# First stage of a fused kernel on one core: differences of the running sums move from GpSimd to ScalarE, and the mask of C B gets two buffers

## What is computed

```python
zxbcdt = x @ W_in;  z, xBC, dt = split(zxbcdt)
xBC = silu(conv4(xBC));  xh, B, C = split(xBC)         # 8 heads of 64, state 64
dt = softplus(dt + dt_bias);  dA = dt * -exp(A_log)
A_cum = cumsum(dA)                                     # per head, along the tokens
L[l, s] = exp(A_cum[l] - A_cum[s])  for l >= s, else 0
Y_diag  = sum_s (C[l] . B[s]) * L[l, s] * (x[s] dt[s])
states  = B, exp(A_cum_last - A_cum), x dt;  h = h * exp(A_cum_last) + states
Y_off   = C . h * exp(A_cum)
Y = (Y_diag + Y_off + D x) * silu(z);  out = rmsnorm(Y) @ W_out @ W_lin + b_lin
```

## Time and profile before

| | |
|---|---|
| median of 3 runs | 2502.82 us |
| profiled execution | 2497.99 us, span 2496.1 us |
| TensorE (PE) busy | 2238.8 us, 90% |
| VectorE (DVE) busy | 1960.6 us, 79% |
| ScalarE (ACT) busy | 1490.8 us, 60% |
| GpSimd (POOL) busy | 1297.5 us, 52% |
| granted TensorE clock, mean | 0.955 of full |
| chain that ended last, by engine | PE 39%, DVE 25%, issue 13%, POOL 12%, ACT 10% |

### The profile page before, as it was taken

The page is one execution under the profiler, slowest core; times in us unless marked ns, Lnnn a source line. Parts: engine busy times, 40 slices in busy tenths (PEclk is TensorE's granted clock), DMA queues, the critical chain, the costliest instruction groups (busy, mean ns, idle before and its releaser), DMA issues.

```text
span 2496.1 us, 25955 instructions
## 1 busy us (share of the span) xinstructions
PE 2238.8 (90%) x8852; PEld 1398.2 (56%) x8852; DVE 1960.6 (79%) x2207; ACT 1490.8 (60%) x2192; POOL 1297.5 (52%) x978
## 2 busy tenths in 40 slices
PE   7997989898989898989898999999999996765998
PEld 4443545454545444545766666666666673433886
DVE  5677878787878876422889898999989898896765
ACT  4676666666667563324575766666675756663444
POOL 2104343434252516330988888888787888791000
PEclk9998999999999999999999999999999998687999
DMA  5332232323232333223323233332323321112121
GB/s 208 98 112 95 97 108 91 114 81 118 76 118 85 110 100 103 84 70 127 110 94 117 87 116 96 104 117 90 114 86 119 102 76 34 43 51 102 42 75 44
DMA packets 116309, 238.05 MB, mean 95 GB/s; under 512 B 8226, under 2 KB 65954, under 8 KB 115794
## 3 DMA queue, kind: packets, MB, share of 16 engines
q1 hardware_dynamic: 107106, 204.00, 25.2%
q0 software_dynamic: 8528, 31.36, 3.5%
q10 hardware_dynamic: 544, 1.05, 0.1%
HBM read 216.06 MB, written 20.32 MB: 95 GB/s over the span
## 4 chain that ended last, share of the span: by engine, by line
PE 39%; DVE 25%; issue 13%; POOL 12%; ACT 10%; DMA 0%; DVEq 0%; POOLq 0%; SPq 0%; ACTq 0%
PE ps L633 9%; POOL dB L2248 8%; DVE h L1430 6%; DVE wgt L1098 4%; PE ps L675 3%; DVE wgt L1105 3%; PE ps L797 2%; DVE acc L1402 2%; PE ps L919 2%; ACT wgt L1617 2%; ACT th L1617 2%; ACT ps L1617 2%; DVE cc L1177 2%; POOL acc L2231 2%; POOL du L2244 2%
## 5 line engine op out<-in xcount | busy, mean ns | idle before, releaser
L2248 POOL TENSOR_TENSOR dB<-du,bc 128x512 f32<-128x512 f32 x512 | 656.8, 1301 | 90.9 <-DVE h L1430 87.5
L1430 DVE TENSOR_TENSOR_SCAN h<-ps,hst,dB 128x512 f32<-128x512 f32 x512 | 643.6, 1272 | 45.7 <-ACT ps L1617 37.6
L1617 ACT ACTIVATE ps<-dt,cols 128x512 f32<-128x512 f32 x512 | 351.4, 687 | 269.6 <-DVE h L1430 267.8
L633 PE MATMUL ps<-wgt,msg 128*128 128x512 f32 x1024 | 501.8, 605 | 9.3 <-DVE wgt L1105 7.8
L675 PE MATMUL ps<-raw,msg 128*128 128x256 f32 x1792 | 452.9, 389 | 0.9 <-ACT hb L1617 0.9
L919 PE MATMUL ps<-consts,h 128*128 128x128 f32 x2048 | 335.5, 291 | 97.1 <-DVE acc L1402 53.6
L919 PEld LDWEIGHTS ps<-consts,h 128*128 128x128 f32 x2048 | 255.4, 148 | 270.4 <-DVE acc L1402 112.7
L675 PEld LDWEIGHTS ps<-raw,msg 128*128 128x128 f32 x1792 | 331.6, 196 | 74.4 <-issue 39.3
L633 PEld LDWEIGHTS ps<-wgt,msg 128*128 128x128 f32 x1024 | 191.1, 195 | 218.7 <-issue 201.9
L1617 ACT ACTIVATE wgt<-wgt 128x1024 f32<-128x1024 f32 x256 | 258.8, 1048 | 79.3 <-DVE wgt L1098 77.7
L2231 POOL TENSOR_TENSOR acc<-acc,part 128x512 f32<-128x512 f32 x160 | 210.5, 1315 | 79.7 <-ACT part L1617 76.2
(11 more groups left out here) (325 smaller groups left out, 3631.8 us busy)
## 6 DMA issues: line engine op xcount, KB each, us to landing
raw<-in_adjT SPq DMA_DIRECT2D x256, 512.0 KB, 3.6
bc<-tmp_bc SPq DMA_DIRECT2D x64, 512.0 KB, 4.8
E<-tmp_bc POOLq DMA_DIRECT2D x32, 512.0 KB, 4.0
xb<-in_xT POOLq DMA_DIRECT2D x8, 512.0 KB, 4.2
tmp_x<-xb POOLq DMA_DIRECT2D x8, 512.0 KB, 3.1
x<-tmp_x SPq DMA_DIRECT2D x8, 512.0 KB, 4.9
tmp_x<-x SPq DMA_DIRECT2D x8, 512.0 KB, 3.6
raw<-tmp_xn SPq DMA_DIRECT2D x8, 512.0 KB, 4.0
```

The costliest lines, as they stand in the source:

```text
L633: x = e.matmul(P[d][:, :], msg[:, j, d * 128:(d + 1) * 128], wgt[g % NW][:, l, :], start=j == 0, stop=j == NJ - 1)
L1430: e.tensor_tensor_scan(hr[n % 3][:, m, :], PS[4 + k % 2].t[:, :], dBr[k % 4][:, :], hst[:, n % 16, m:m + 1], ALU.mult, ALU.add).then_inc(S ...
L1617: return e.activation(out, in_, func, bias=bias, scale=scale)
L2248: e.tensor_tensor(dBr[k % 4][:, :], du[:, m, :], bcr[i % 3][:, n % 2, :], ALU.mult).then_inc(S("dB"), 1)
```

## The change

On ScalarE, the two GpSimd operations on E become one Relu for each head: relu(A_cum[s] - A_cum[l]) with scale -1 and the column of A_cum[s] as bias, in place; Exp then runs with scale -1. The eight Relus come in two groups of four, one step of the order apart, the second together with Exp. GpSimd's L2126 and L2128 are gone, with the semaphore `cut`. `cbm` has two buffers, and VectorE waits for the M of the chunk two back.

```diff
-        cbm = sb(cA, "cbm", [128, 128])
+        cbms = [sb(cA, f"cbm{i}", [128, 128]) for i in range(2)]
...
-                    w.wait_ge(S("M"), c)
-                    e.tensor_tensor(cbm[:, :], b.ps[:, 128:256], tri, ALU.mult).then_inc(b.evac, 1)
+                    w.wait_ge(S("M"), c - 1)
+                    e.tensor_tensor(cbms[s % 2][:, :], b.ps[:, 128:256], tri, ALU.mult).then_inc(b.evac, 1)
...
-                        w.wait_ge(S("cut"), 8 * (ib - 1))
+                        w.wait_ge(S("E"), 9 * 4 * (ib - 1))
...
                     yield from (None, None)
+
+                    w.wait_ge(S(f"d_E{c % 3}"), 16 * (c // 3 + 1))
+                    w.wait_ge(S("sums_a"), ib + 1)
+                    for h in range(8):
+                        x = E[c % 3][:, h, :]
+                        act(x, x, ACT.Relu, scale=-1.0, bias=sums_a[p][:, 0, s, h:h + 1]).then_inc(S("E"), 1)
+                        if h == 3:
+                            yield
                     x = E[c % 3][:, :, :].rearrange("p h l -> p (h l)")
-                    w.wait_ge(S("cut"), 2 * c + 2)
-                    act(x, x, ACT.Exp).then_inc(S("E"), 1)
-                    yield from (None, None)
+                    w.wait_ge(S("E"), 9 * c + 8)
+                    act(x, x, ACT.Exp, scale=-1.0).then_inc(S("E"), 1)
+                    yield
...
-                    x = E[c % 3][:, :, :]
-                    w.wait_ge(S("sums_a"), ib + 1)
-                    w.wait_ge(S(f"d_E{c % 3}"), 16 * (c // 3 + 1))
-                    e.tensor_tensor(x, x, sums_a[p][:, 0, s, :, None].broadcast_to([128, 8, 128]), ALU.subtract).then_inc(S("cut"), 1)
-                    w.wait_ge(S("cut"), 2 * c + 1)
-                    e.tensor_scalar(x, x, 0.0, None, ALU.min).then_inc(S("cut"), 1)
...
-                    w.wait_ge(S("E"), c + 1)
+                    w.wait_ge(S("E"), 9 * c + 9)
```

More of the change, by code:

```diff
@@ L2139, in inner @@
                     yield from (None, None)
-                    w.wait_ge(S("E"), c + 1)
+                    w.wait_ge(S("E"), 9 * c + 9)
                     w.wait_ge(inner_use(ib, s, 1).evac, inner_use(ib, s, 1).n)
-                    e.tensor_tensor(E[c % 3][:, :, :], E[c % 3][:, :, :], cbm[:, None, :].broadcast_to([128, 8, 128]),
+                    e.tensor_tensor(E[c % 3][:, :, :], E[c % 3][:, :, :], cbms[s % 2][:, None, :].broadcast_to([128, 8, 128]),
                                     ALU.mult).then_inc(S("M"), 1)
```

## The result

The changed kernel took 2477.59 us (median of 5 runs, 2469.23 to 2482.45), the kernel before beside it 2497.54 (5 runs, 2494.07 to 2504.38). The ratio is 0.9913 [0.9885, 0.9941], some 22 us less (20 by these two medians). The forecast was 2460 with a range from 2440 to 2490: the direction and the range hold, but of the 43 us forecast about half came.

The account below looks back on a forecast made before the run. TensorE, 93% busy in the first stage, was taken as the bound, its idle time the prize. Blocks 1 to 5 27.8, block 0 2.9, block 6 6.5 and 2, block 7 4: 43.2 us off 2497.99, plus 4.8, gives 2460 (2440 to 2490).

Parts of the forecast that it names:

- the replay: Block start, new order worked through on old times: L586's 5.04 us wait goes, 5.7 us won at each start.
- so its two run from 716.85 to 719.2 (1.17 each): Block start: the two L1105 need e2, meet M 0, then run at 1.17 us each; xc follows at 720.4.
- the half clock: Granted clock 0.50 (1.2 GHz, not 2.4) behind L586's wait; forecast to go with it, some 3.1 us.
- the 1.8 extra of one of them: L586's waits in blocks 1 to 5: five of 5.03 us plus 1.8 extra in one, added to the gain.
- TensorE, at full clock, wants xc: Block start: TensorE wants xc for L693 at 718.2, gets it at 720.5; 2.3 of 8.1 us become new waits.
- start 0: Start of block 0: its 2.9 us wait at L586 goes; the clock is low there already.
- In chunk 3 e1 stands before the Relus: Mid-block: reason, with ScalarE idling later in the block, for charging the Relus' delay only 0.5 us a block.
- I give its going nothing: Removing GpSimd's minimum: one tensor input, L1098 and L1177 run through it with little added, so no gain counted.
- start 6: Start of block 6: earlier Square and free L1149 cut TensorE's 7.17 us wait; 5.5 + 1.0 = 6.5 us won.
- eaten in mid-block: Rival, chance 0.18: Relus delay e1 and e2, waits at L755 and L788 grow 4.2 us a block; 2482 us.
- Slower: Rival, chance 0.07: ScalarE becomes the chain, a block losing 11.6 us against 5.7 won; 2520 us.
- More is kept: Rival, chance 0.15: M 0 meets neither L1105 nor L1153, 2.3 us more at five starts; 2448 us.

Follow-up runs that it names:

- e4_one_input: Kernel before, with GpSimd's two-input subtraction replaced by a longer one-input addition of 0.0: 2479.11 us, ratio 0.991.
- e5_late_first: Changed kernel, with chunk 0's Relus and Exp moved behind e2 and the norm's Ln and Exp on ScalarE: 2452.77 us, ratio 0.9814.
- e9_decay_first: e5_late_first, with GpSimd's state decay hd of a chunk ahead of the next chunk's M: 2434.65 us, ratio 0.9752 to the kernel before.
- e13_no_relu_late: e9_decay_first without the Relus, so difference and cut are not computed: 2437.03 us, ratio 0.9769 to the kernel before.
- e8_hole: e3_no_relu, with a one-input GpSimd instruction (xdec times 1.0) between xdec and M: 2459.83 us, ratio 0.9848 to the kernel before.
- e2_one_mask: Changed kernel with one cbm mask again, VectorE waiting for the M of the chunk before: 2488.68 us, ratio 0.9946 to the kernel before.
- e3_no_relu: Changed kernel without the eight Relus, so difference and cut are not computed: 2481.07 us, ratio 0.9921 to the kernel before.
- e6_per_head_pool: Kernel before, with subtraction and minimum fused on GpSimd into one one-input instruction per head: 2491.93 us, ratio 0.9974.

## Why the prediction was half right

**The mechanism: right.** VectorE's L1149 was held by GpSimd's two-input subtraction; with it gone L1149 takes 0.69 and the waits of L586 at five starts are gone. That it is the meeting that costs, and not the amount of GpSimd's work, is shown by e4_one_input (GpSimd 56 us busier, kernel faster) and by e5_late_first and e9_decay_first, which take away nothing. That the number of inputs matters rests on rows in which a pair of VectorE instructions runs beside a one-input one (2.35 to 2.57 us) or is held by two-input ones (up to 8.05).

**The price of a Relu: nearly.** One takes 382 to 394 ns, over the 0.35 that the prediction gave as a sign of being wrong, but the sum uses the time from one to the next. Four take 1.26 and eight 2.44, so that is 0.29 instead of 0.26, inside the bounds. The estimate by the Trainium skill ("ScalarE: Activation LUTs", section "What ACT_TABLE_LOAD costs") was 0.29, and the trace agrees with it. It didn't decide: e13_no_relu_late, without them, is no faster than e9_decay_first. In the order of the kernel after, the Relus do make L1105 wait for e2 (1.51 at the start, 1.31 in mid-block), and e5_late_first gets most of that back by their place alone.

**The start of a block: right as far as it was replayed, and stopped too early.** From the first L1098 on, the replay had L1149 at 2.6 us and M 0 at 4.8; they came at 2.6 and 4.9. It had L693 at 10.8, and it came at 11.9 (before: 16.5). The step that failed here is "so its two run from 716.85 to 719.2 (1.17 each)". It let L1105 meet M 0, but `xdec` of chunk 1 stands on GpSimd right behind M 0, and it held the second L1105 for its 1.05 us. So 4.6 us come in at this start, not 5.7.

**One start taken for all.** The prediction read the cost of the half clock, 3.1 us, at the start at 718. From L586 to L693 that start takes 8.2 us, the longest of the five; the others take 8.1, 7.9, 7.0 and 7.1, and at full clock it is 5.2 (e5_late_first). On average 2.5 us were to be won there, not 3.1, and the five starts gave 22.6 us in all, 4.5 each, with the 1.8 extra of one of them already in it.

**The clock: the step that failed and cost most.** "TensorE, at full clock, wants xc": the replay took the half clock as gone with the wait of L586. It moved. Behind the waits of 1.34 and 1.50, L755, L633 and L760 take 1.38, 1.91 and 1.65 for two, where two at full clock take 1.02 to 1.10: 1.8 us. It is so behind all five starts (0.50 in the two microseconds from 360, 480, 599, 718 and 838), and 1.7 us longer behind start 0. The prediction noted that 2.3 us of new waits would come and priced them at their length alone.

**The middle of a block: charged too low.** "In chunk 3 e1 stands before the Relus" is true of e1, but e2 stands behind them. In the kernel after:

```profile
755.74 2.38 POOL L2143 TENSOR_TENSOR E<-E,cbm 128x1024 f32<-128x1024 f32 x1 [3.69 <-ACT E L1617]
...
757.13 4.06 DVE L1105 SCALAR_TENSOR_TENSOR wgt<-raw,wgt 128x1024 f32<-128x1024 f32 x2 [1.31 <-ACT wgt L1617]
...
758.05 2.05 POOL L2155 TENSOR_TENSOR hd<-hs,ecd 64x512 f32<-64x512 f32 x1
...
762.97 1.13 PE L755 MATMUL ps<-hs,cc 128*128 128x512 f32 x2 [1.37 <-DVE hs L1232]
```

The same shape as at the start: L1105 late for e2, then held by M 3 and `hd`. The wait at L755 is 1.37 where before it was 0.61: 0.8 instead of 0.5. With the 1.8 of the clock that is the 2.6 us by which each stretch between two starts is slower. So a block gains 4.5 - 2.6, or 1.9 us (119.5 instead of 121.4 from start 1 to start 5), and 1.6 on average with the slower first stretch. Of the 19.7 us that are missing in these five blocks, 12.0 are missing between the starts, nearly all of it the half clock, and 7.7 at the starts.

**Removing the minimum: "I give its going nothing" didn't look at its place.** The minimum was the one-input instruction between GpSimd's two-input ones, and in the kernel before the pair L1105 (718.85, 2.34 us) runs inside it unhindered:

```profile
717.48 3.08 POOL L2128 TENSOR_SCALAR E<-E 128x1024 f32<-128x1024 f32 x1
```

With it gone the two-input ones stand closer together. e8_hole puts a one-input instruction between two others of them and wins 18 us; that the minimum in its old place was worth anything was not tried. What the whole change did to the two VectorE operations shows in two groups of rows (246 to 967, busy us and mean ns), of before, then of after:

```profile
L1098 DVE SCALAR_TENSOR_TENSOR wgt<-wgt 128x1024 f32<-128x1024 f32 x91 | 152.2, 1712 | 18.0 <-ACT wgt L1617 18.0
L1105 DVE SCALAR_TENSOR_TENSOR wgt<-raw,wgt 128x1024 f32<-128x1024 f32 x92 | 108.9, 1224 | 0.2
```

```profile
L1105 DVE SCALAR_TENSOR_TENSOR wgt<-raw,wgt 128x1024 f32<-128x1024 f32 x92 | 131.1, 1465 | 15.6 <-ACT wgt L1617 15.5
L1098 DVE SCALAR_TENSOR_TENSOR wgt<-wgt 128x1024 f32<-128x1024 f32 x91 | 120.6, 1364 | 32.9 <-ACT wgt L1617 32.9
```

L1098 is held 32 us less and L1105 22 us more. The blocking went from one instruction of VectorE to another; some 9 of 32 us are truly gone.

**The mask: needed, but its hold was priced too high.** 3 us at each of five starts would be 15; e2_one_mask shows some 8, of which its trace shows 0.8 a start as longer waits and 2.4 behind start 5, where the clock is low.

**Start 0, start 6 and the rest.** Start 0 gave 3.8 for 2.9. Start 6 gave the 6.5 that were forecast (17.4 to 10.9 us from L582 to L693, with a wait of 2.0 left at L586); the stretch shows 3.9 because the work before it, from start 5 on, is 2.6 slower, which the sum had not charged. The wait at L755 in block 6, of which 2 us were to go, stayed at about 4.1; the rest of the stage gave 4.8 for 6, nearly all of it in block 7, as forecast (4).

**The rivals.** The time is nearest to that of "eaten in mid-block" (2482), but its mechanism isn't what happened: waits at L755 and L788 were to grow by 4.2 a block and grew by 0.8. "Slower" fell with the result itself, and e13_no_relu_late shows that ScalarE is no chain in the best order. "More is kept" named the right place, M 0 against L1105; e5_late_first takes that collision away and gains 25 us, not the 12 that the prediction gave it, as the half clock goes too.

**The base.** The 4.8 us added for the median of the first three runs were their chance: five runs gave 2497.5. It was a lucky error: without it the forecast would have been 2455, 23 us under the result instead of 18. The forecast as a ratio was 0.983, and 0.991 was measured.

## What to carry to other kernels

Where VectorE and GpSimd both run instructions with two SBUF inputs, write down both engines' orders behind every instruction that is moved or removed, and ask of each VectorE instruction on the path which GpSimd ones can run back to back in front of it: here the order alone gave 40 us on top of the change (e9_decay_first). When a wait of TensorE goes and leaves a smaller one, don't count the half clock as won: here 1.8 us a block came back behind waits of 1.34 and 1.50. And read what the clock costs at every repetition, not at one. An instruction that looks like waste on an idle engine may be the gap in which another engine works; ask what closes up when it goes.

## What the runs showed of the hardware that was not expected

**A VectorE instruction with two SBUF inputs gets no turn between GpSimd instructions with two inputs that follow each other.** In e3_no_relu one L1105 (1.2 us of work) waits through `xdec`, M 1 and `hd`, 4.4 us. The holding works the other way too: M takes 2.89 there when L1149 (0.68) starts 0.02 us ahead of it, 2.36 else. The Trainium skill ("SBUF — State Buffer", section "SBUF: two separate sides") says that the shared port pair is an exclusive lock that one instruction holds whole; the trace agrees with that for instructions of two inputs.

**A one-input GpSimd instruction doesn't hold it.** L1098 twice in 2.35 us inside the minimum of e4_one_input, and in 2.36 inside the eight of e6_per_head_pool; L1105 twice in 2.57 inside the addition of e4_one_input. The same section of the Trainium skill counts every GpSimd instruction that reads SBUF against a two-input VectorE one; the measurement differs from it, and decides.

**The half clock doesn't follow the length of a wait.** In e4_one_input the same wait of 3.11 at L586 was followed by a clock of 1.00 at two starts and of 0.50 at three, once for 5 us and more. In the kernel before the wait of 5.03 or 5.04 was followed by 7.0 to 8.2 us from L586 to L693, 5.2 at full clock, and in the kernel after 1.34 and 1.50 by 3 us at 0.50. What of the work around them makes the difference was not tried and stays open.
